# A two-layer graph network on one core: layer one takes three gathers per block, sums in four row groups, and copies on ScalarE in one instruction each

## The reference, cut to what matters

```
h = relu(layernorm(x));  x1 = x + h @ Ws.T + bs + mean over links(h[src] @ Wn.T + bn)
h = relu(layernorm(x1)); out = x1 + relu(sum over links(h[src] * dis[src] * dis[dst]))
dis = count of links to a node, to the power -1/2
```

## Time and profile before

| | |
|---|---|
| median of 3 runs | 1207.74 us (1206.85 to 1208.07) |
| the profiled execution | 1204.19 us, its span 1202.2 us |
| busy share of the span | ScalarE 89%, VectorE 86%, GpSimd 72%, TensorE 71% |
| layer one, 100 to 700 us | TensorE's granted clock 1.00, DMA share about 0.67 |
| layer two, 740 us to the end | granted clock 0.50, DMA share about 0.87 |
| chain that ended last | GpSimd 37%, issue 23%, ScalarE 19%, TensorE 7%, VectorE 7%, DMA 4% |

### The profile page before, as it was taken

How to read it: one execution, slowest core, us unless ns; L and a number is a source line. 1 busy time by engine, 2 the same in 40 slices (tenths; PEclk the granted TensorE clock), 3 DMA queues, 4 the chain that set the end, 5 groups by cost and what they waited for, 6 DMA issues and landing times.

```text
span 1202.2 us, 30432 instructions
## 1 busy us (share of the span) xinstructions
PE 849.3 (71%) x9310; PEld 783.0 (65%) x9408; DVE 1036.2 (86%) x2798; ACT 1067.9 (89%) x2780; POOL 869.7 (72%) x1133
## 2 busy tenths in 40 slices
PE   1589999999999999999899972444444444444444
PEld 1478999999989898888889861433333434334333
DVE  7899999989989989899988735888888888888886
ACT  2589999999999999999999945888888988889896
POOL 4777777777777777777777418777777777777771
PEclk9799999999999999999999995555555555555555
DMA  6346666666666666676666434888888889888894
GB/s 207 119 118 194 210 213 192 214 196 203 196 198 193 214 189 210 183 202 199 196 211 189 147 132 165 257 268 277 259 277 267 262 275 266 274 274 261 264 277 184
DMA packets 82230, 259.38 MB, mean 216 GB/s; under 512 B 19986, under 2 KB 20356, under 8 KB 82116
## 3 DMA queue, kind: packets, MB, share of 16 engines
q1 hardware_dynamic: 58948, 210.86, 55.4%
q0 software_dynamic: 22400, 46.91, 14.1%
q10 hardware_dynamic: 768, 0.20, 0.1%
HBM read 152.93 MB, written 104.37 MB: 214 GB/s over the span
## 4 chain that ended last, share of the span: by engine, by line
POOL 37%; issue 23%; ACT 19%; PE 7%; DVE 7%; DMA 4%; POOLq 2%; ACTq 0%; DVEq 0%
POOL X L694 30%; ACT work L804 11%; DMA X<-in_x,IDX 3%; ACT area L814 3%; ACT area L819 3%; PE p_O L984 2%; PE p_O L996 2%; POOL work L647 2%; POOL work L631 2%; POOL work L651 2%; PE p_T L959 1%; DVE ST L1419 1%; DVE area L1481 1%; ACT sd L776 1%; POOL factor L667 1%
## 5 line engine op out<-in xcount | busy, mean ns | idle before, releaser
L804 ACT ACTIVATE work<-X,shift,scale 128x128 f32<-128x128 f32 x1329 | 550.2, 518 | 2.0 <-DVE shift L1456 1.8
L694 POOL DMA_INDIRECT X<-in_x,IDX x392 | 389.2, 993 | 130.4 <-issue 97.3
L1419 DVE BATCH_NORM_STATS2 ST<-X 128x6 f32<-128x256 f32 x1176 | 409.4, 415 | 39.0 <-DMA X<-in_x,IDX 36.9
L1047 PE MATMUL p_O<-work 32*128 32x128 f32 x1984 | 205.4, 435 | 222.3 <-POOL work L635 138.8
L694 POOL DMA_INDIRECT X<-x_table,IDX x294 | 286.5, 975 | 93.2 <-issue 91.1
L1047 PEld LDWEIGHTS p_O<-work 32*128 32x128 f32 x1984 | 178.0, 323 | 242.8 <-issue 188.1
L804 ACT ACTIVATE p_O<-X,shift,scale 128x128 f32<-128x128 f32 x496 | 201.2, 444 | 25.4 <-DVE area L1503 23.1
L984 PE MATMUL p_O<-wnT,area 128*128 128x128 f32 x1568 | 217.6, 282 | 4.6 <-DVE area L1481 4.4
L996 PEld LDWEIGHTS p_O<-wsT,area 128*128 128x128 f32 x1568 | 206.8, 192 | 7.4
L996 PE MATMUL p_O<-wsT,area 128*128 128x128 f32 x1568 | 207.5, 275 | 5.2
L984 PEld LDWEIGHTS p_O<-wnT,area 128*128 128x128 f32 x1568 | 191.5, 192 | 7.3 <-DVE area L1481 7.2
(11 more groups left out here) (175 smaller groups left out, 1114.7 us busy)
## 6 DMA issues: line engine op xcount, KB each, us to landing
x_table<-area SPq DMA_DIRECT2D x98, 528.0 KB
X<-x_table SPq DMA_DIRECT2D x98, 528.0 KB
X<-in_x SPq DMA_DIRECT2D x98, 512.0 KB, 4.3
out_x<-area SPq DMA_DIRECT2D x98, 512.0 KB, 5.8
X<-in_x,IDX POOLq DMA_INDIRECT x392
X<-x_table,IDX POOLq DMA_INDIRECT x294
moved<-held SPq DMA_DIRECT2D x32, 12.2 KB
es<-in_src SPq DMA_DIRECT2D x1, 488.5 KB, 3.6
```

What stands on the lines that cost most here:

```text
L694: nc.gpsimd.indirect_dma_start(got(s)[:, k, 0:w], None, table, bass.IndirectOffsetOnAxis(ap=IDX[:, s, k:k + 1], axis=0)).then_inc(gathered ...
L804: last = nc.scalar.activation(o, row(l, s, r), ACT.Relu, bias=shift[:, s, r:r + 1], scale=scale[:, s, r:r + 1])
L1047: ends[half] = nc.tensor.matmul(outs1[p][g][:, c], SEL[1][q, p, part_of, :], H[1][q, p, draw, :], start=False, stop=(half == 1 and part_of ...
L1419: last = V.bn_stats(ST[:, s, r:r + 2, :].rearrange("p r k -> p (r k)"), pair.rearrange("p r c -> p c r"))
```

## The change

Both layers now gather three times per block and share one table layout. `SRC`, `DL` and `DISL` are made in it at once: VectorE spreads each code over four groups of 32 rows (`spread`, in place of `double`), TensorE brings them to their partitions with four small products against `of_block` (`turn_lot`), ScalarE copies them in one instruction (`take_lot`), and `decode` is in three parts, which join the two halves of the shared gather. The dis values go the same way in seven further steps of layer one, 82 to 88. `move_links`, `join_links`, `hold_links`, line 1020, line 870, the sixteen transfers of ScalarE and the waits for them are gone.

In layer one TensorE sums in four groups of 32 partitions, each into a bank of its own: `p_T` now has four banks of two transposes each, and the counts and the table products lie in the fourth beside them. `p_c` is gone, and the outputs have four banks. ScalarE copies a block's eight transposes in one instruction (4 x 256 elements) and its sums with the counts in one (4 x 264); the counts are inverted from that copy. VectorE measures the eleventh row as a pair with itself. ScalarE normalises ten rows of a block, GpSimd the eleventh. Layer two is the same but for the names of the tables and the banks.

```diff
-PAIRS = BT // 2
-ROWS = BT + PAIRS
+QUADS = 4
+PARTS = 4
 DRAWS = 3
-ROWS1 = BT + DRAWS
+ROWS = BT + DRAWS
...
+    def lot_at(k):
+        if k == 2:
+            return 1
+        if DIS_AT < k <= DIS_AT + TB:
+            return TB + k - DIS_AT - 1
+        return next((g for g in BEGIN if BEGIN[g] + 11 == k), None)
+    def tiles(g):
+        return [(a, k, 2 * g + a + QUADS * k) for a in range(2) for k in range(2)]
+    def of_half(v, g):
+        return v.rearrange("p (k c) d -> p c k d", k=2)[:, 2 * g:2 * g + 2, :, :]
...
-        p_T = [ps(f"p_T{g}", [P, GT * P]) for g in range(2)]
-        p_O = [ps(f"p_O{k}", [P, GT * P]) for k in range(BANKS)]
-        p_c = ps("p_c", [P, 512])
+        p_T = ps("p_T", [P, QUADS, 512])
+        p_O = [ps(f"p_O{k}", [P, GT * P]) for k in range(4)]
         p_s, p_n = p_O[0:2], p_O[2:4]
+        counts = p_T[:, QUADS - 1, COUNTS:COUNTS + BT]
+        scratch = p_T[:, QUADS - 1, SCRATCH:TOTALS].rearrange("p (k n) -> p k n", k=PARTS)
...
+            return p_O[2 * (off % 2) + g]
+        outs1 = ((p_O[0], p_O[1]), (p_O[2], p_O[3]), (p_T[:, 0, :], p_T[:, 1, :]), (p_T[:, 2, :], p_T[:, 3, :]))
+        def summed(off, g):
+            return aT[:, off % 2, g, :].rearrange("p (a c) -> p a c", a=2)
...
+            def take_lot(m):
+                act.wait_ge(s_codeT, m + 1)
+                if m < TB:
+                    if m > 0:
+                        act.wait_ge(s_tab, m)
+                    nc.scalar.activation(codeT[:, :, :], scratch, ACT.Copy, bias=TOP, scale=-1.0).then_inc(s_coded, 1)
+                else:
+                    c = slice(GROUP_BLOCKS * (m - TB), GROUP_BLOCKS * (m - TB) + GROUP_BLOCKS)
+                    nc.scalar.copy(DISL[:, :, c], scratch[:, 0:DRAWS, :]).then_inc(s_coded, 1)
...
-            def spill_h(turn, off, g):
+            def spill_h(turn, off):
                 i, _, _ = place(0, turn, off)
-                act.wait_ge(hT_ps, 2 * i + g + 1)
+                act.wait_ge(hT_ps, 2 * i + 2)
                 if not first(i, HT):
-                    act.wait_ge(prod_ready[g], i - HT + 1)
-                nc.scalar.copy(hT[:, off % HT, g, :], p_T[g][:, :]).then_inc(hT_sb, 1)
-
-            def spill_a(turn, off, g):
+                    act.wait_ge(prod_ready[1], i - HT + 1)
+                nc.scalar.copy(hT[:, off % HT, :, :].rearrange("p g (a c) -> p (g a) c", a=2), p_T[:, :, 0:2 * P]
+                               ).then_inc(hT_sb, 1)
+            def spill_a(turn, off):
                 i, _, _ = place(0, turn, off)
                 act.wait_ge(aT_ps, i + 1)
-                nc.scalar.copy(aT[:, off % 2, g, :], p_T[g][:, :]).then_inc(aT_sb, 1)
+                nc.scalar.copy(aT[:, off % 2, :, :].rearrange("p g (a c) -> p (g a) c", a=2), p_T[:, :, 0:2 * P + BT]
+                               ).then_inc(aT_sb, 1)
...
-                    spill_h(turn, off, 0)
-                    spill_h(turn, off, 1)
+                    spill_h(turn, off)
                 if there(0, turn, off - 3):
                     dis(turn, off - 3)
                 if starting:
                     for i in due(off, ROOT_AHEAD):
                         root0(turn, i)
                 if there(0, turn, off + 1):
-                    normalise(0, turn, off + 1, range(0, MID if joins_at(off) is None else CODES_AFTER))
-                if joins_at(off) is not None:
-                    take_codes(joins_at(off))
-                    normalise(0, turn, off + 1, range(CODES_AFTER, MID))
+                    normalise(0, turn, off + 1, range(0, MID))
...
                 if there(0, turn, off):
-                    spill_a(turn, off, 0)
-                    spill_a(turn, off, 1)
+                    spill_a(turn, off)
+                if lot_at(off) is not None:
+                    take_lot(lot_at(off))
...
                 if there(0, turn, off + 1):
                     normalise(0, turn, off + 1, range(MID, ROWS if not own_rows(off + 1) else ROWS - 1))

...
+            def turn_lot(m):
+                pe.wait_ge(s_codes, m + 1)
+                if m > 0:
+                    pe.wait_ge(s_coded, m)
+                for k in range(PARTS):
+                    to = k if m < TB else min(k, DRAWS - 1)
+                    last = nc.tensor.matmul(scratch[:, to, :], codes4[:, k, :], of_block[:, :], start=(to == k),
+                                            stop=(m < TB or k != DRAWS - 1), skip_group_check=True)
+                last.then_inc(s_codeT, 1)
...
-                    pe.wait_ge(aT_sb, 2 * i + g - 1)
-                for j in range(GT):
-                    last = nc.tensor.matmul(p_T[g][:, P * j:P * j + P], H[0][:, off % HR[0], GT * g + j, :], ident[:, :],
-                                            start=(j == 0), stop=False, is_transpose=True, skip_group_check=True)
+                    pe.wait_ge(aT_sb, i)
+                if g == 1 and lot_at(off - 1) is not None:
+                    pe.wait_ge(s_coded, lot_at(off - 1) + 1)
+                for a, k, j in tiles(g):
+                    last = nc.tensor.matmul(p_T[:, 2 * g + a, P * k:P * k + P], H[0][:, off % HR[0], j, :], ident[:, :],
+                                            start=(k == 0), stop=False, is_transpose=True, skip_group_check=True)
                 last.then_inc(hT_ps, 1)
...
+                pe.wait_ge(hT_sb, i + 1)
+                for k in range(DRAWS):
+                    for q in range(QUADS):
+                        of = slice(HALF * q, HALF * q + HALF)
+                        c = slice(P * k, P * k + P) if k < DRAWS - 1 else slice(0, 2 * P)
+                        part_of = SEL[0][of, p, k, :] if k < DRAWS - 1 else SEL[0][of, p, k:PARTS, :].rearrange("p a n -> p (a n)")
+                        nc.tensor.matmul(p_T[:, q, c], H[0][of, p, BT + k, :], part_of, start=False,
+                                         stop=(k == DRAWS - 1), skip_group_check=True)
+                if lot_at(off) is not None:
+                    turn_lot(lot_at(off))
...
-                for j in range(GT):
-                    for g in range(2):
-                        q = slice(SLOTS * g, SLOTS * g + SLOTS)
-                        nc.tensor.matmul(p_T[g][:, P * j:P * j + P], H[0][q, p, BT + j, :], SEL[0][q, p, j, :],
-                                         start=False, stop=(j == GT - 1), skip_group_check=True)
-                if joins is not None:
-                    pe.wait_ge(s_coded, joins + 1)
-                if off == SUM_AT:
-                    pe.wait_ge(s_total_read, 1)
-                for j in range(PAIRS):
-                    c = 2 * j
-                    nc.tensor.matmul(p_c[:, c:c + 2], SEL_high[:, p, j, :, 1], halves[:, :], start=(j == 0), stop=False,
+                for k in range(PARTS):
+                    c = slice(QUADS * (k % 2), QUADS * (k % 2) + QUADS)
+                    nc.tensor.matmul(counts[:, c], SEL_high[:, p, k, :, 1], quarters[:, :], start=(k == 0), stop=False,
                                      skip_group_check=True)
-                last = nc.tensor.matmul(p_c[:, 0:BT], ones3[:, :], parts1[:, :], start=False, stop=True,
+                last = nc.tensor.matmul(counts, ones3[:, :], parts1[:, :], start=False, stop=True,
                                         skip_group_check=True)
                 last.then_inc(aT_ps, 1)
             def neighbours(turn, off, g):
                 i, _, _ = place(0, turn, off)
-                back, used = divmod(g + 1, 2)
-                if not first(i, 3 - back):
-                    pe.wait_ge(prod_used[used], i - 2 + back)
-                if off == 1 and g == 1:
+                if not first(i, 2):
+                    pe.wait_ge(prod_used[g], i - 1)
+                if off == 1 and g == 0:
                     pe.wait_ge(s_prod_read, 1)
-                pe.wait_ge(aT_sb, 2 * i + g + 1)
-                for j in range(GT):
-                    c = slice(P * j, P * j + P)
-                    last = nc.tensor.matmul(out0(off, g)[:, c], aT[:, off % 2, g, c], wnT[:, :],
-                                            start=(j == 0), stop=False, skip_group_check=True)
+                pe.wait_ge(aT_sb, i + 1)
+                for a, k, _ in tiles(g):
+                    c = 2 * a + k
+                    last = nc.tensor.matmul(out0(off, g)[:, P * c:P * c + P], summed(off, g)[:, a, P * k:P * k + P], wnT[:, :],
+                                            start=(c == 0), stop=False, skip_group_check=True)
                 last.then_inc(n_ready[g], 1)
...
+            def spread(m, values):
+                if m > 0:
+                    dve.wait_ge(s_codeT, m)
+                for k in range(PARTS):
+                    of = (slice(0, HALF), slice(0, HALF), slice(HALF, SLOTS), slice(SLOTS - 1, HALF - 1, -1))[k]
+                    c = slice(QUADS * (k % 2), QUADS * (k % 2) + QUADS)
+                    last = V.scalar_tensor_tensor(
+                        codes4[:, k, :].rearrange("p (q n) -> p q n", q=QUADS),
```

(22 more changed lines are left out.)

335 lines of the change are left out of this document (113 added, 222 removed).

## The result

The changed kernel took 1234.72 us (median of 4 runs, 1233.94 to 1235.74); the kernel before took 1207.9 on the same chip. The ratio is 1.0224, 95% interval 1.0206 to 1.0241: 2.2% slower, where 1188 us was forecast. The profiled span is 1232.1 us, 29.9 more than before.

A forecast was written before the change was run, and what follows sets the result against it. Layer one was bound by four engines within 5% (ScalarE 6.44 us a block), layer two by GpSimd. 86 x 6.28 plus 6, 2.5 and 5 is 553.6 against 572.4; with changeover -0.8, total -19.6: 1188 us, range 1173 to 1210.

The forecast's parts named there:

- Steps with tables: Twelve layer-one steps between blocks 10 and 96: eight extra TensorE passes, 0.5 us a step (bounds 0.2 and 0.9), 6 us.
- long VectorE instructions: VectorE's long reciprocal and scans in layer one: TensorE now notices them through fewer output banks, 2.5 us by estimate.
- rival 3: Layer one: with four output banks late gathers delay products, sums and ScalarE; changeover included +12 us, 1220 us; chance 0.09.
- The pace: Layer one, blocks 10 to 96: 6.28 us a block (bounds 6.22 to 6.40), 540.1 us for 86 blocks.
- Loop (a): Layer one: joined copies chain transposes, their copy, eight rows and sums copy into 6.28 us, equal to TensorE's own work.
- Rival 4: Layer one: a copy over four banks costs more than its elements; 0.3 us more each gives 1220 us; chance 0.05.
- Start: Block 0 to 10: longer decoding and joined waits, paid for by one row and a code copy less: 0 us.
- the waits for rows: VectorE's waits for gathered rows in layer one would fall under 10 us.
- a reserve: GpSimd in layer one: one gather less leaves 5.17 us of work, 1.1 us of reserve per block.
- ScalarE's idle: Layer one: ScalarE idle 0.2 to 0.3 us per block, released by transposes.
- The changeover: Between layer one and layer two: TensorE's turning of the seven tables goes, -0.8 us.
- jitter: Layer one: 5 us kept for late gathers and jitter that margins of 0.05 to 0.4 us don't hold.

The follow-up runs named there:

- two_codes: The changed kernel with two buffers instead of one for the table on its way to TensorE: 1197.02 us, ratio 0.9934 to the kernel before.
- halves: The kernel of two_codes with each joined ScalarE copy (transposes, sums) split in two again, each side waiting for its own half: 1191.42 us, ratio 0.989.
- joined_before: The kernel before with only the joined ScalarE copies of transposes and of sums, each side waiting for the whole: 1207.77 us against 1205.76, ratio 1.0016.
- two extra operations: The kernel of two_codes plus two unused 128x128 maximum operations on GpSimd in each block of layer one: 1197.89 us, ratio 0.9948.
- the fourth gather: The kernel of two_codes plus a gather of 128 rows into a spare tile per layer-one block, which the statistics await: 1212.2 us, ratio 1.006.
- turn_after: The kernel of halves with TensorE turning a table behind the counts instead of ahead of them: 1191.62 us, ratio 0.9901.

## Why the prediction was wrong

1. **The step that failed is "Steps with tables".** It counted the late tables' products (0.5 us each) and long VectorE instructions, and no wait. The diff has one: `spread` waits for the turning of the lot before, through a single buffer. The kernel before had this wait too (`double`), for tables 14 blocks apart; new are seven tables in consecutive blocks. The earlier trace rows held one side of the ring: the addition at 213.89 releases the products at 214.95 with 0.4 us to spare. I used that margin for rival 3 and did not ask what else could come between VectorE and its addition. No rival named this wait either. The measured term is 36.9 us. The miss is 46.7 by the medians (1234.7 against 1188) and 49.5 by the spans (1232.1 against 1182.6), since the forecast put the median 3.55 above the profiled execution and it is 0.8 above.
2. The same step, sizes: in `two_codes` a code table costs 0.8 us over two steps (6.50 and 7.08, against 6.37 each) and a late one 0.8 (7.18), 9.9 for twelve and not 6. I gave the eight passes 0.07 each by the sums' passes, but those run in different rows of the array and these fill 112 rows: from 595.50 to the counts at 596.41 it is 0.91 / 8 = 0.114 each, though they have 14 columns. The Trainium skill (TensorE: Matmul & The Clock Gate, LDWEIGHTS (loading the stationary operand)) has the load of weights take the time of its columns, not of its rows. The trace agrees: the weights here are of 112 rows and 128 columns, and their passes come no faster than those of L945 with 128 rows (592.31 to 593.21, 0.113 each), though the products behind them have 14 columns against 128. The blocks with the reciprocal and the scans (78 and 80) were 2.0 us over the pace, 2.5 were forecast.
3. **The pace, 6.37 and not 6.28** (7.3 us over 86 blocks). Loop (a) was the right mechanism. Term by term, from the rows at 203.43 to 209.80: transposes to the copy 1.10 (forecast 1.09), copy to dis 0.91 (0.90), dis 0.11, rows 3.08, sums copy to transposes 1.17 (1.10). The last hop is the miss. `halves` opens the loop and finds TensorE's 6.28. Rival 4 (dear copies) is out: four banks in one copy take 1.01 us in the mean, and two banks in `joined_before` 1.01 and 1.00. To the next instruction the joined copies are 0.91 and 0.92 us (forecast 0.90 and 0.93); the Trainium skill (ScalarE: Activation LUTs, What ACT_TABLE_LOAD costs) had them at 0.95 and 0.97; the trace does not agree, and the measured ones decide.
4. **Start, +5.8 and not 0 (bounds -3 and +3).** 2.0 us are the joined waits (`halves` gives them back). 2.6 us are there before any block is summed: the first gather starts at 30.57 and not 27.95. That is the table form: the eight passes of the first lot take 1.88 us behind 16.7 us without work (1.06 later on), where one transpose took 0.45 before, and the decoding is longer. The last 1.2 us were not traced.
5. Right: the waits for rows ended, and GpSimd has a reserve (0.74 us idle a block at its last row and 0.48 in the longer instruction there, 1.1 forecast); why the rows had been late is shown only in part (above). Rival 3 did not come, since there are no late gathers to hand on. ScalarE's idle 0.26 a block is released by transposes. Layer two is 484.6 us from its first gather (485 forecast, 485.1 before). The changeover was forecast at -0.8; from the sums copy of block 96 to that gather it is -0.35 (19.04 us against 19.39).
6. Without the stall the miss would have been 12.8 us (the span of `two_codes` is 1195.4, that of the forecast 1182.6): the start's 5.8 and the pace's 7.3. What comes on top of the pace between blocks 10 and 96 is 13.3 us where 13.5 were forecast, and that is in part luck: the tables 9.9 against 6, the long instructions 1.9 against 2.5, and 1.5 in four blocks that come behind code tables against the 5 kept for jitter.

## What to carry to other kernels

When a change shares a buffer between steps, write down for each new wait what its engine has queued behind it, and follow that until it comes back or ends; a ring through a second engine's queue costs a whole period per turn, though both waits look short. Put a wait that may be long at the place in the step where the engine's next instruction waits for the same thing anyway: that one move was worth as much as a second buffer. And before splitting or joining copies, look at whether the two sides overlap in halves: joining saved ScalarE nothing that it needed and closed a loop.

## What the runs showed of the hardware

**TensorE's clock is lower behind waits of 3.45 us.** In the stall the granted clock of the changed kernel goes up and down with every turn (columns: window, length, busy time and instructions of PE, PEld, DVE, ACT and POOL, clock, DMA share, GB/s):

```profile
604.00:610.00 6.00, 5.11 (x62) 4.53 (x60) 0.96 (x5) 5.04 (x11) 1.53 (x2) 0.99 0.21 74
610.00:617.00 7.00, 4.43 (x20) 4.28 (x21) 5.42 (x14) 1.36 (x5) 3.18 (x4) 0.57 0.50 156
617.00:624.00 7.00, 5.42 (x61) 4.84 (x60) 1.66 (x7) 5.74 (x14) 0.95 (x1) 0.94 0.09 26
```

It is at the upper of its two levels (2.4 GHz) in the stretches of 0.94 and 0.99, and mostly at the lower one (1.2 GHz) in that of 0.57, behind the wait; the eight products that take 1.06 to 1.14 elsewhere took 1.54 at 600.13 and 2.07 at 612.57. The waits themselves stay at 3.45; from the products to the next turning it is 7.80 us in the first turn (600.13 to 607.93) and 8.93 in the fourth (639.34 to 648.27). That is the rise from 12.44 to 13.6 us a turn.

**GpSimd and VectorE get into each other's way.** GpSimd's first instruction of the last row takes 0.45 us, and 0.93 at 208.01 above, where it started beside VectorE's comparison (0.68 us, two operands in SBUF). In the changed kernel, between 110 and 500 us, 55 of 61 ran into that comparison and took 0.86 in the mean; the other six took 0.45. In eight of the 55 GpSimd had started 0.2 us ahead, and in seven of these it kept its 0.45, and the comparison took 0.78. The Trainium skill (SBUF — State Buffer, SBUF: two separate sides) has the two share a pair of ports as an exclusive lock, held by whichever starts first, against VectorE's instructions with two SBUF operands. The trace agrees that one of the two gets longer, and mostly the later. By the pace it cost nothing here, since GpSimd had the time.

**Another chip was 7 to 15% slower**, by the kernel: before 1375.66 against 1205, two extra operations 1307.22 against 1197.89, the fourth gather 1391.49 against 1212.2, `turn_after` 1273.11 against 1191.62. Most instructions took the same (in the kernel with two operations a gather 0.98 and 0.99 us, the statistics 0.415 and 0.417), and the granted clock between 200 and 500 was 1.00 on both; from block 97 to the end it was 555.5 us against 498.6, with 240 GB/s against 269 between 850 and 1100. So it is not the engines' own speed; the transfers are the likely cause, which was not tested. The kernels with three gathers lose less there: `turn_after`, the change with its stall out and its copies halved, is 7.4% faster than the kernel before on that chip and 1.0% on this. The change with two buffers alone did not run there.
